# Filter products moved from POOL to VectorE, x loaded first, and additions, norms and routing of the first half rearranged in a two-layer attention and mixture-of-experts kernel

## The chip, the cores and the metric

One core of a Trainium2 chip runs the whole program. Its engines are TensorE (PE; PEld are its weight loads), VectorE (DVE), ScalarE (ACT), GpSimd (POOL) and SyncE (SP), which issues most DMAs. The metric is the device time of one execution in microseconds, less is better. Three runs of the kernel before took 493.38, 490.51 and 492.42 us, the median is 492.42.

## The reference

Two layers on x of 4 x 1024 x 128, all float32. Cut to what matters:

```python
xn = layernorm(x)
x = x + attention(xn, w_q, w_k, w_v) + moe_top1(xn, wg, W, b)      # layer 0
xn = layernorm(x)
x = x + conv(xn, Wu, Wv, W1, W2, W3, Wo) + moe_top2(xn, Wg, W1, W2) # layer 1
```

Attention is causal, with rotated q and k, one head of 128, four sequences of 1024. `moe_top1` sends each token to the best of 8 experts (128x128 each, 512 tokens at most), `moe_top2` to the best two of 8 experts (128 to 256 to 128, relu). `conv` is a long convolution over 1024 positions by FFT: `y = (xn Wu + bu) * irfft(rfft(xn Wv + bv) * rfft(h))`, then `Wo`. Its filter h comes from positions alone, h = gelu(gelu(pos W1 + b1) W2 + b2) W3 + b3 with a decay, where gelu(v) is taken as 0.5 v (1 + tanh(c (v + 0.0447 v^3))).

## The kernel before

The 4096 tokens are 32 tiles of 128 (`NT`), 8 per sequence (`J`), and `i` or `n` is mostly a tile. Every engine has one program written out by hand; they meet only at semaphores, and each engine takes its instructions in order. Nothing is scheduled by a planner: tables of row numbers at the top of the file (lines 165 to 184 and 226 to 227) say behind which row of attention a piece of other work stands.

Prelude. SP loads x in four groups, the constants, `wvg` (weights of values and of layer 0's gates), the transform matrices `mats`, `wqk`, `rope`, layer 0's expert weights and biases, and then fills the DRAM tables `slots0`, `moe0` and `slots1` with markers (L702, L707). VectorE takes statistics of each group and writes normalized rows (L1482, L1485, L1491); between them POOL computes the inverse deviation by a power (`inverse_std`, L798 and L800). PE transposes the rows, ACT copies them to `xT`, PE multiplies by `wvg`, ACT copies values and gate logits out (`take_values`). The filter's two hidden layers are spread over the prelude: PE multiplies (`filter_layer`), ACT makes a biased copy and a square (L956, L959), POOL makes `ht = ht*hx + hx` as a multiplication and an addition (`times_x_plus_x`, L847), ACT the tanh (L963), POOL `hg = hg*hx + hx`; that is four times two POOL instructions of 64x1024. Then VectorE runs `routing0`: one-hots of the best expert, the count of earlier tokens by two matmuls on PE (`routing_counts`), the slot of each token (`slot0`, last written at L1546).

Rows. With the slots POOL scatters the 32 tiles of rows to `slots0` (`scatter_rows`, L826), one indirect DMA each, waiting after every second. Meanwhile PE, ACT and VectorE go through attention, row block n = 0 to 31: PE `scores(n+1)`; VectorE `row_max(n+1)` (L1713, L1717); ACT `exp_rows(n+1)` (L1010); PE `transpose_probs(n)` (L1263); ACT and VectorE copy them (L1020, L1725); PE `weigh_values(n-1)`; VectorE `attention_row(n-1)` adds to x (L1731). Rotated q and k of the next sequence come in between (`project` on PE, `rotate` on VectorE), and so do pieces of other work:

- The filter's last layer at row 2, its radix pass on VectorE (`radix_forward`) in rows 3 to 5, its spectrum on PE (`filter_spectrum`, 64 matmuls in two rows) in rows 6 and 7.
- Layer 0's experts from row `MOE0_FROM` = 8: when all 32 scatters are in, SP loads the sorted rows (L715) into a ring of 16, PE transposes and multiplies (L1297, L1305), VectorE adds the bias (L1739), POOL sends each tile back to its tokens (`send_back`, L836). When all 32 are back, SP loads them (`y0`, L736).
- From row 21 on VectorE adds them to x and takes statistics for the second norm, tile by tile (`add_tiles`, L1747, L1751, L1755; `ADD_BEFORE_MAX` and `ADD_BEHIND_ROW`). POOL computes the deviations of groups 0 to 2 right away (L880 to L888). ACT writes normalized rows of these groups (`norm_rows`, L1027, `NORM_AT`), PE transposes them (`transpose_norms`, L1281) and multiplies by the gate weights (`gates`, `GATES_AT`). The last group's rows are written by VectorE (L1491), four and four.
- The first half of the tokens (tiles 0 to 15) is routed to layer 1's experts in pieces between rows 26 and 28 (`routing1`, 30 steps). After it POOL scatters them with `dispatch` (L813): 16 tiles for the best expert, new ids (`second_ids`, L822), 16 tiles for the second best. In front of dispatches 4 and 12 of this scatter stand the two halves of the last group's deviation (`NORM_IN_SCATTER`, four tiles each).

After the rows PE works off a list, `conv_at(PRELUDE)`: projections of the convolution, `("vu", k)`, five of them, then the transposes of the last group's normalized rows, three more projections, that group's gates, four projections, the counts of the second routing, the rest, and eight forward transforms. VectorE has, in this order: the last group's second four rows (`norm_rows(2 * B - 1, J // 2, J // 2)`, waiting for `rstd_done`), ten steps of the first radix pass, the second half's routing up to its one-hots, the rest of the radix pass, the rest of the routing, eight spectral products. POOL scatters the second half of the tokens: 12 dispatches (`SCATTER_IN_PRELUDE`) ahead of the expert rounds, two per round later. SP loads rows for the rounds once the first half's scatter is in. Then come 40 rounds of a pair of expert tiles each, with the inverse transforms between them, and a tail that adds everything and stores.

## Time and profile before

| | before |
|---|---|
| median of three runs | 492.42 us |
| the profiled execution | 493.04 us |
| its span, first to last instruction | 491.2 us |
| mean granted clock of PE | 0.934 of full |
| PE busy | 366.0 us, 75% |
| PEld busy | 298.7 us, 61% |
| VectorE busy | 294.4 us, 60% |
| POOL busy | 258.4 us, 53% |
| ACT busy | 225.9 us, 46% |

Busy shares are averages over stages that have different limits, and the idle time of an engine that isn't the bottleneck costs nothing. "Idle before <-releaser" in a row tells how long the engine had stood still before the instruction and whose work ended that wait. Matmul ends are modelled, and POOL's spans are rough. All helper matmuls have one line, L1161, so they are told apart by their tiles.

### The profile page before, as it was taken

To read this page: it belongs to the slowest core of one execution; us is meant where nothing else is said; L and a number is where in the kernel's file an instruction comes from. 1 tells how busy PE (TensorE), PEld (TensorE's weight loads), DVE (VectorE), ACT (ScalarE), POOL (GpSimd) and SP (SyncE) were. 2 spreads that over 40 slices of the span, in tenths; PEclk is the share of its full clock that TensorE was granted. 3 is DMA by queue.
4 is the path that set the end of the run, shared out by engine and by line. 5 is a ranking of instruction groups with operands and counts; after the bars stand their busy time and mean duration, and the time that the engine had idled before them with its cause. 6 is when DMAs were issued, how large, how long until landed. Compare 5 with 4: busy or idle time off the path is not lost.

```text
span 491.2 us, 7805 instructions
## 1 busy us (share of the span) xinstructions
PE 366.0 (75%) x2302; PEld 298.7 (61%) x2302; DVE 294.4 (60%) x782; ACT 225.9 (46%) x551; POOL 258.4 (53%) x254
## 2 busy tenths in 40 slices
PE   2485588869997975949997978898887777766720
PEld 0272255658675644737996867787776667755620
DVE  3977569614773796474688993478438772244105
ACT  1373042325332316334343066434567676687724
POOL 2754766733666323016566676666666555365540
PEclk9999599997998999687998999999999999999975
DMA  9999999823321330001111282445322215422407
GB/s 211 396 197 262 166 140 135 268 51 85 87 75 40 111 89 1 1 5 39 34 34 37 69 261 75 142 140 151 112 69 75 63 29 158 137 74 74 126 11 252
DMA packets 64744, 55.05 MB, mean 112 GB/s; under 512 B 6819, under 2 KB 56683, under 8 KB 64446
## 3 DMA queue, kind: packets, MB, share of 16 engines
q1 hardware_dynamic: 57888, 41.71, 35.6%
q0 software_dynamic: 6656, 12.51, 8.4%
q10 hardware_dynamic: 158, 0.33, 0.4%
q8 instruction: 19, 0.31, 0.3%
q14 instruction: 23, 0.19, 0.1%
HBM read 30.44 MB, written 25.27 MB: 113 GB/s over the span
## 4 chain that ended last, share of the span: by engine, by line
PE 44%; issue 13%; ACT 12%; DVE 10%; DMA 10%; POOL 8%; SPq 1%; ACTq 0%; POOLq 0%; DVEq 0%
PE psS L1161 19%; PE psO L1161 15%; PE psT L1161 7%; ACT hT L1122 7%; POOL slots L826 4%; DMA slots<-row,slot 4%; DMA moe<-ys,xs 2%; POOL w L847 2%; DMA xres<-in_x 2%; ACT row L1027 1%; PE psT L1263 1%; POOL moe L836 1%; DVE work L1713 1%; DVE xres L1747 1%; DMA moe<-ys,ring 1%
## 5 line engine op out<-in xcount | busy, mean ns | idle before, releaser
L813 POOL DMA_INDIRECT slots<-row,slot x64 | 69.3, 1083 | 57.0 <-DVE slot L1580 22.4
L836 POOL DMA_INDIRECT moe<-ys,xs x61 | 61.1, 1001 | 58.3 <-issue 16.6
L1161 PE MATMUL psO<-ring,hT 128*128 128x128 f32 x320 | 45.2, 284 | 45.1 <-ACT hT L1122 45.1
L1161 PEld LDWEIGHTS psO<-ring,hT 128*128 128x128 f32 x320 | 38.7, 191 | 53.4 <-issue 53.4
L1122 ACT ACTIVATE hT<-psT,ring 128x128 f32<-128x128 f32 x160 | 45.6, 368 | 45.7 <-PE psT L1161 45.7
L1868 DVE TENSOR_TENSOR ys<-psO,ring 128x256 f32<-128x256 f32 x40 | 17.0, 424 | 75.3 <-PE psO L1161 75.1
L1055 ACT ACTIVATE ring<-w 128x642 f32 x80 | 55.9, 761 | 1.1 <-issue 1.0
L1161 PE MATMUL psS<-work 128*128 128x512 f32 (+3 forms) x96 | 42.6, 558 | 12.6 <-DVE work L1696 8.8
L836 POOL DMA_INDIRECT moe<-ys,w x35 | 38.0, 1087 | 23.3 <-DVE ys L1868 9.7
L1020 ACT ACTIVATE work<-psT 128x512 f32<-128x512 f32 (+3 forms) x32 | 16.5, 516 | 66.6 <-PE psT L1263 66.6
L826 POOL DMA_INDIRECT slots<-row,slot x32 | 34.9, 1091 | 18.1 <-DMA slots<-row,slot 10.9
L1161 PE MATMUL psT<-xsT,ring 128*128 128x128 f32 x320 | 42.3, 275 | 0.5 <-ACT xsT L1115 0.5
L1161 PEld LDWEIGHTS psT<-xsT,ring 128*128 128x128 f32 x320 | 39.9, 192 | 1.3 <-ACT xsT L1115 0.7
L1161 PE MATMUL psO<-work 128*128 128x128 f32 x288 | 39.7, 286 | 0.0
L1010 ACT ACTIVATE work<-psS,work 128x128 f32<-128x128 f32 (+7 forms) x32 | 23.7, 739 | 34.7 <-DVE work L1717 34.4
L1713 DVE TENSOR_REDUCE work<-psS 128x1 f32<-128x128 f32 (+7 forms) x32 | 24.0, 750 | 25.5 <-PE psS L1161 23.9
L1161 PEld LDWEIGHTS psO<-work 128*128 128x128 f32 x288 | 37.1, 203 | 0.0
L1161 PEld LDWEIGHTS psS<-work 128*128 128x128 f32 x96 | 17.9, 214 | 27.5 <-issue 18.5
L1263 PE MATMUL psT<-cst,work 128*128 128x128 f32 x144 | 24.0, 298 | 14.3 <-ACT work L1010 14.3
L1161 PE MATMUL psS<-xT,work 128*128 128x512 f32 x64 | 31.1, 628 | 1.3 <-ACT work L1010 1.3
L1263 PEld LDWEIGHTS psT<-cst,work 128*128 128x128 f32 x144 | 17.0, 153 | 23.2 <-ACT work L1010 18.3
L1161 PE MATMUL psS<-work,mats 128*128 128x256 f32 x128 | 30.1, 395 | 0.0
(272 smaller groups left out, 781.4 us busy)
## 6 DMA issues: line engine op xcount, KB each, us to landing
slots<-xs SPq DMA_DIRECT2D x14, 516.0 KB, 14.7
mats<-in_iv SPq DMA_DIRECT2D x16, 256.0 KB, 3.7
xs<-slots SPq DMA_DIRECT2D x61, 64.5 KB, 1.9
w<-in_w SPq DMA_DIRECT2D x8, 321.0 KB
w<-slots SPq DMA_DIRECT2D x35, 64.5 KB, 1.9
xres<-in_x SPq DMA_DIRECT2D x4, 512.0 KB, 9.7
mats<-in_fw SPq DMA_DIRECT2D x1, 2048.0 KB, 11.3
moe<-xs SPq DMA_DIRECT2D x4, 512.0 KB, 7.8
```

Of the source, the lines that this page charges most:

```text
L813: pool.indirect_dma_start(slots1[:, :], bass.IndirectOffsetOnAxis(ap=(slot1, slot2)[k][:, i:i + 1], axis=0), row[:, i, :], None, bounds_ch ...
L826: pool.indirect_dma_start(dst[:, :], bass.IndirectOffsetOnAxis(ap=slots[:, i:i + 1], axis=0), row[:, i, :], None, bounds_check=bound, oob_ ...
L836: pool.indirect_dma_start(dst[:, :], bass.IndirectOffsetOnAxis(ap=row_slots[l][m][:, D:ROWW].bitcast(I32), axis=0), ys[:, n % UNROLL, :], ...
L847: pool.tensor_tensor(t[0:FO, :], t[0:FO, :], hx[0:FO, :], op).then_inc(f_pool, 1)
L1010: act.activation(prob[n % 2][:, 0:(i + 1) * P], S[n % 2][:, :, :].rearrange("p a m -> p (a m)")[:, 0:(i + 1) * P], ACT.Exp, bias=negmax[:, ...
L1020: act.activation(pT[n % 2][:, 0:k, :].rearrange("p j q -> p (j q)"), t_bank("p", n, 0)[:, 0:k * P], ACT.Copy).then_inc(pt_act, 1)
L1055: act.activation(pair_w[p % RING_PAIRS][:, t, :], w12[:, bass.ds(e, 1), :].rearrange("p e h -> p (e h)"), ACT.Copy).then_inc(e_w, 1)
L1122: last = act.activation(hT[:, k, :], TP[1][:, k * P:(k + 1) * P], ACT.Relu, bias=pair_w[p % RING_PAIRS][:, k // 2, B1_AT + k % 2:B1_AT + k ...
L1161: return pe.matmul(o, lhsT, rhs, start=start, stop=stop)
L1263: last = pe.transpose(t_bank("p", n, c)[:, (j - 4 * c) * P:(j - 4 * c + 1) * P], prob[n % 2][:, j * P:(j + 1) * P], ident)
L1713: dve.tensor_reduce(negmax[:, n:n + 1], S[n % 2][:, :, :].rearrange("p a m -> p (a m)")[:, 0:(n % J + 1) * P], X, ALU.max, negate=True).th ...
L1868: tt(ys[:, m:m + 2, :], O[p % 2][:, 0:2 * D].rearrange("p (t d) -> p t d", d=D), pair_w[p % RING_PAIRS][:, :, B2_AT:W_COLS], ALU.add).then ...
```

## The change

The two filter layers leave the prelude. PE's matmuls for them, ACT's three activations and the products now stand in rows 0 to 4 (`FILT_AT`), and the products are four fused instructions on VectorE, (ht + 1) * hx and (hg + 1) * hx. Radix pass and spectrum follow in rows 6 to 8 and in rows 9 and 10, the experts of layer 0 start at row 9. SP loads all of x before `wvg`, puts `w0`, its biases and the matrices behind the first fills, and layer 1's weights behind the first 16 loads of sorted rows, the second eight of which now wait for the filter's radix pass. PE makes projection (0,0) between token groups 1 and 2, VectorE rotates it and takes row 0's maximum in the middle of the first routing. At the other end the additions of tiles 0 to 15 come in two blocks of eight, those of 16 to 23 move to rows 26 and 27, norms of groups 0 and 1 stand in rows 22 and 23, their transposes ahead of the row's own (`TOKENS_AT`), gates in rows 23 and 24; the first half's routing has 12 steps behind row 24, 10 behind row 25 and the rest ahead of row 27's maximum. On POOL the third group's norm and both halves of the last one stand in front of dispatches 6, 14 and 24 of the scatter, and 20 dispatches of the second half stand ahead of the rounds.

```diff
-FILT_RADIX_AT, FILT_DFT_AT = 3, 6
-
-SPLIT_AT = 9
-GATES_AT = (24, 25, 29)
-NORM_AT = {23: [(0, 0), (0, 1)], 24: [(1, 0), (1, 1)], 27: [(2, 0)], 28: [(2, 1)]}
-COUNTS_AT = 27
+FILT_AT = (0, 2)
+FILT_RADIX_AT, FILT_DFT_AT = 6, 9
+
+SPLIT_AT = 12
+TOKENS_AT = (23, 24, 29)
+GATES_AT = (23, 24, 29)
+NORM_AT = {22: [(0, 0), (0, 1)], 23: [(1, 0), (1, 1)], 28: [(2, 0), (2, 1)]}
+COUNTS_AT = 25
...
-MOE0_FROM = 8
+MOE0_FROM = 9
...
-ADD_BEFORE_MAX = {22: (4, 8), 23: (12, 16), 25: (20, 24), 29: (24, 28), 31: (28, 30)}
-ADD_BEHIND_ROW = {21: (0, 4), 22: (8, 12), 24: (16, 20)}
-ROUTING_BEFORE_MAX = {26: 6, 28: 8}
-ROUTING_BEHIND_ROW = {26: 6, 27: 10, 28: R1_STEPS}
+ADD_BEFORE_MAX = {22: (8, 16), 27: (20, 24), 29: (24, 28), 31: (28, 30)}
+ADD_BEHIND_ROW = {21: (0, 8), 26: (16, 20)}
+ROUTING_BEFORE_MAX = {26: R1_STEPS}
+ROUTING_BEHIND_ROW = {24: 12, 25: 10}
...
-SCATTER_IN_PRELUDE, SCATTER_PIECES = 12, 2
-NORM_IN_SCATTER = (4, 12)
+SCATTER_IN_PRELUDE, SCATTER_PIECES = 20, 2
+NORM_IN_SCATTER = (6, 14, 24)
...
-                    sp.dma_start(wvg, wvg_in).then_inc(w_a_loaded, 16)
-            sp.dma_start(mats[:, :, :, :], fw_in).then_inc(fw_loaded, 16)
+            sp.dma_start(wvg, wvg_in).then_inc(w_a_loaded, 16)
             sp.dma_start(wqk, wqk_in).then_inc(rope_loaded, 16)
             sp.dma_start(rope, rope_in).then_inc(rope_loaded, 16)
-            sp.dma_start(w0[:, :, :], w0_in).then_inc(moe0_w_loaded, 16)
-            sp.dma_start(y0.rearrange("p j d -> p (j d)"), b0_in.rearrange("e d -> (e d)").partition_broadcast(P)).then_inc(moe0_w_loaded, 16)
-            sp.dma_start(bias[:, :], bvuo_in.partition_broadcast(P)).then_inc(bias_loaded, 16)
...
             fill_slots(0, slots0, TILES0)
             for i in range(0, NT, 8):
                 sp.dma_start(moe0[i * P:(i + 8) * P, :].rearrange("(i p) w -> p i w", p=P),
                              xs[:, :, 0:D]).then_inc(moe0_filled, 16)
+            sp.dma_start(mats[:, :, :, :], fw_in).then_inc(fw_loaded, 16)
             fill_slots(1, slots1, TILES1)
...
-            sp.wait_ge(rad_f, RAD_F)
-            for a, b in [(w12[:, e, :], w12_in[e]) for e in range(E)] + [
-                    (wv[:, :], wv_in), (wu[:, :], wu_in), (wg1[:, :], wg1_in), (wo[:, :], wo_in)]:
-                sp.dma_start(a, b).then_inc(l1_w_loaded, 16)
-
-
             sp.wait_ge(slots_filled[0], 16 * TILES0 // 8)
             sp.wait_ge(moe0_filled, 16 * NT // 8)
             sp.wait_ge(slots_filled[1], 16 * TILES1 // 8)
             sp.wait_ge(sent0, 16 * NT)
             for n in range(TILES0):
+                if n == UNROLL:
+                    sp.wait_ge(rad_f, RAD_F)
                 load_rows(0, slots0, n)
+                if n == RING[0] - 1:
+                    for a, b in [(w12[:, e, :], w12_in[e]) for e in range(E)] + [
+                            (wv[:, :], wv_in), (wu[:, :], wu_in), (wg1[:, :], wg1_in), (wo[:, :], wo_in)]:
+                        sp.dma_start(a, b).then_inc(l1_w_loaded, 16)
...
-            inverse_std(0)
-            inverse_std(1)
-            filter_cubic(0)
-            inverse_std(2)
-            inverse_std(3)
-            filter_gelu(0)
-            filter_cubic(1)
-            filter_gelu(1)
+            for g in range(B):
+                inverse_std(g)
...
-            for g in range(B - 1):
+            def second_norm(g):
+
                 tiles = slice(J * g, J * g + J)
                 inverse_std(B + g)
...
 
+            second_norm(0)
+            second_norm(1)
             pool.wait_ge(ids_done, 2)
             pool.wait_ge(xn_done, NT + NT // 2)
             pool.wait_ge(slots_filled[1], 16 * TILES1 // 8)
             pool.wait_ge(slot1_ready, 2)
+            def norms_in_scatter(j):
+
+                if j == NORM_IN_SCATTER[0]:
+                    second_norm(2)
+                if j in NORM_IN_SCATTER[1:]:
+                    inverse_std(2 * B - 1, J // 2 * (NORM_IN_SCATTER.index(j) - 1), J // 2)
+
             for i in range(HT):
-                if i in NORM_IN_SCATTER:
-                    inverse_std(2 * B - 1, J // 2 * NORM_IN_SCATTER.index(i), J // 2)
+                norms_in_scatter(i)
                 dispatch(0, 0, i)
             for g in range(2):
                 second_ids(0, g)
             pool.wait_ge(ids_done, 4)
             for i in range(HT):
+                norms_in_scatter(HT + i)
                 dispatch(0, 1, i)
...
             exp_rows(0)
             for n in range(NT):
+                if n in TOKENS_AT:
+                    g = TOKENS_AT.index(n)
+                    for u in (2 * g, 2 * g + 1):
+                        take_transposed(u, t_bank("t", u))
                 take_pt(n)
                 if n + 1 < NT:
                     exp_rows(n + 1)
+                if n in FILT_AT:
+                    act.wait_ge(filt_loaded, 32)
+                    filter_layer(FILT_AT.index(n))
+                if n - 1 in FILT_AT:
+                    filter_tanh(FILT_AT.index(n - 1))
...
-            pe.wait_ge(filt_loaded, 32)
-            filter_layer(0)
             pe.wait_ge(cst_loaded, 16)
             pe.wait_ge(w_a_loaded, 16)
             for g in range(B):
                 transpose_tokens(g)
                 values_and_gates(g)
+                if g == 1:
+                    pe.wait_ge(rope_loaded, 32)
+                    project(0, 0)
             pe.wait_ge(casts_done, 3)
             pe.wait_ge(ones_done, 2)
-            filter_layer(1)
+            scores(0)
             pe.wait_ge(vg_free, 16)
             routing_counts(0, O[0])
-            pe.wait_ge(rope_loaded, 32)
-            pe.wait_ge(f_act, 4)
-            project(0, 0)
-            pe.wait_ge(rt, R0_CUM)
-            scores(0)
+            pe.wait_ge(filt_loaded, 32)
             for n in range(NT):
                 for b, h in projections_at(n):
                     project(b, h)
                 if n + 1 < NT:
                     scores(n + 1)
+                if n in FILT_AT:
+                    filter_layer(FILT_AT.index(n))
+                if n in TOKENS_AT:
+                    g = TOKENS_AT.index(n)
+                    for u in (2 * g, 2 * g + 1):
+                        wait_emptied(pe, T_USES, T_AT[("t", u)])
+                        transpose_norms(u, t_bank("t", u))
                 transpose_probs(n)
                 if n == FILT_RADIX_AT - 1:
                     filter_layer(2)
                 if n in (FILT_DFT_AT, FILT_DFT_AT + 1):
                     for u in range(2):
                         filter_spectrum(2 * (n - FILT_DFT_AT) + u)
+                if n == 1:
+                    pe.wait_ge(rt, R0_CUM)
                 if n:
                     weigh_values(n - 1)
...
+            def filter_cubic(k):
+                dve.wait_ge(f_act, 3 * k + 2)
+                stt(ht[0:FO, :], ht[0:FO, :], 1.0, hx[0:FO, :], ALU.add, ALU.mult).then_inc(f_dve, 1)
+
+            def filter_gelu(k):
+                dve.wait_ge(f_act, 3 * k + 3)
+                stt(hg[0:FO, :], hg[0:FO, :], 1.0, hx[0:FO, :], ALU.add, ALU.mult).then_inc(f_dve, 1)
...
+            norm_stats(0)
+            norm_stats(1)
+            norm_rows(0)
+            norm_stats(2)
+            norm_rows(1)
+            norm_stats(3)
+            norm_rows(2)
+            norm_rows(3)
 
             def rotate(b, h):
 
@@ -1761,12 +1762,21 @@
 
             dve.wait_ge(rope_loaded, 32)
             rotate(0, 0)
+            dve.wait_ge(vg_free, 16)
+            dve.wait_ge(cst_loaded, 16)
+            first_layer_routing = routing0()
+            take(first_layer_routing, R0_OH)
+            row_max(0)
+            finish(first_layer_routing)
...
             for n in range(NT):
                 for b, h in projections_at(n):
                     rotate(b, h)
+                if n - 1 in FILT_AT:
+                    filter_cubic(FILT_AT.index(n - 1))
+                if n - 2 in FILT_AT:
+                    filter_gelu(FILT_AT.index(n - 2))
```

Not shown: PE's, ACT's and the bank tables' bookkeeping, by which the filter's two layers use score bank 0 in turn with the rows and the transposes take their banks ahead of the row's.

## Rows read from the trace of the kernel before

**Rows 1.** The page's chain that ended last, shares of the span by engine.

```profile
PE 44%; issue 13%; ACT 12%; DVE 10%; DMA 10%; POOL 8%; SPq 1%; ACTq 0%; POOLq 0%; DVEq 0%
```

**Rows 2.** Groups by line, POOL, 0 to 54 us: count, busy us and mean ns, idle before.

```profile
L847 POOL TENSOR_TENSOR w<-w 64x1024 f32<-64x1024 f32 x8 | 18.7, 2339 | 11.5 <-ACT w L959 10.0 <-ACT w L963 1.2
```

**Rows 3.** Timeline, 0 to 56 us: start us, us, instruction, idle before and releaser.

```profile
38.34 0.59 DVE L1513 TENSOR_REDUCE m<-lg 128x32 f32<-128x256 f32 x1 [4.77 <-ACT lg L951]
...
41.62 3.60 PE L1161 MATMUL psS<-xT,work 128*128 128x512 f32 x8
...
44.94 2.07 DVE L1542 SCALAR_TENSOR_TENSOR tables<-tables 128x256 f32<-128x256 f32 x1
...
47.50 0.42 DVE L1544 SCALAR_TENSOR_TENSOR tables<-tables 128x256 f32<-128x256 f32 x1
...
48.58 1.69 DVE L1546 TENSOR_SCALAR slot<-best 128x32 int32<-128x32 f32 x1
...
52.84 1.52 POOL L826 DMA_INDIRECT slots<-row,slot  x1 [0.19 <-issue]
```

**Rows 4.** Timeline of PE, 88 to 120 us.

```profile
97.62 3.81 PE L1161 MATMUL psT<-hspec,mats 128*128 128x128 f32 x32 [0.34 <-ACT work L1020]
...
108.83 0.45 PE L1297 MATMUL psT<-cst,xs 128*128 128x128 f32 x1 [3.44 <-DMA xs<-slots]
```

**Rows 5.** Timeline of POOL, 100 to 265 us, the sends back.

```profile
117.53 0.97 POOL L836 DMA_INDIRECT moe<-ys,xs  x1 [11.91 <-DVE ys L1739]
...
164.74 0.97 POOL L836 DMA_INDIRECT moe<-ys,ring  x1 [0.30 <-issue]
```

**Rows 6.** Timeline of DVE, 118 to 200 us, additions and maxima.

```profile
171.81 1.13 DVE L1747 SCALAR_TENSOR_TENSOR xres<-work,gate,xres 128x128 f32<-128x128 f32 x4
...
177.49 1.13 DVE L1747 SCALAR_TENSOR_TENSOR xres<-work,gate,xres 128x128 f32<-128x128 f32 x4
...
179.60 1.19 DVE L1713 TENSOR_REDUCE work<-psS 128x1 f32<-128x1024 f32 x1
...
185.88 0.26 DVE L1713 TENSOR_REDUCE work<-psS 128x1 f32<-128x128 f32 x1
```

**Rows 7.** Timeline of DVE, 197 to 292 us, the first routing's first step.

```profile
204.08 0.37 DVE L1513 TENSOR_REDUCE m<-lg 128x16 f32<-128x128 f32 x1 [3.50 <-ACT lg L1036]
```

**Rows 8.** Timeline of POOL, 100 to 265 us, the second scatter.

```profile
218.78 1.12 POOL L813 DMA_INDIRECT slots<-row,slot  x1 [22.37 <-DVE slot L1580]
...
240.27 0.23 POOL L798 TENSOR_SCALAR veps<-mv 128x4 f32<-128x4 f32 x1 [2.87 <-DVE mv L1755]
240.65 1.04 POOL L800 TENSOR_TENSOR rstd<-veps,cst 128x4 f32<-128x4 f32 x1
...
248.24 0.42 POOL L822 COPY row<-cst 128x8 int32<-128x8 int32 x1
```

**Rows 9.** Timeline of DVE, 236 to 252 us.

```profile
241.73 1.12 DVE L1491 TENSOR_SCALAR row<-xres,mv,rstd 128x128 f32<-128x128 f32 x4 [1.65 <-POOL rstd L800]
...
251.96 0.37 DVE L1513 TENSOR_REDUCE m<-lg 128x16 f32<-128x128 f32 x1 [1.48 <-ACT lg L1036]
```

**Rows 10.** Timeline of PE, 197 to 292 us.

```profile
244.88 1.04 PE L1281 MATMUL psS<-cst,row 128*128 128x128 f32 x8
...
249.76 1.85 PE L1161 MATMUL psS<-wg,xT 128*128 128x8 f32 x16
...
281.08 0.40 PE L1417 MATMUL psT<-cst,xs 128*128 128x128 f32 x2
```

**Rows 11.** Timeline of SP, 80 to 290 us.

```profile
278.53 1.80 SPq L715 DMA_DIRECT2D xs<-slots  x4
```

**Rows 12.** Timeline of PE, 118 to 200 us, gates after an idle stretch.

```profile
194.20 3.55 PE L1161 MATMUL psO<-wg,xT 128*128 128x8 f32 x16 [3.44 <-ACT xT L1032]
```

**Rows 13.** Windows: stretch, us, busy us of PE, PEld, DVE, ACT, POOL, granted clock, DMA, GB/s.

```profile
194.00:196.00 2.00, 1.80 (x9) 1.83 (x9) 0.00 (x0) 0.54 (x2) 1.81 (x2) 0.51 0.00 0
```

**Rows 14.** Timeline of POOL, 70 to 93 us.

```profile
81.78 1.93 POOL L826 DMA_INDIRECT slots<-row,slot  x1 [0.78 <-DMA slots<-row,slot]
```

57 lines of the change are left out of this document (15 added, 42 removed).

## Prediction

> **What bounds the kernel now.** I read first the page's chain that ended last [rows 1]: TensorE (PE) and its hand-overs carry most of it, and POOL's scatter with its DMAs a good tenth. That is an average over stages, so I walked the chain in order of time and looked in each stage, on each engine's timeline, for the wait that ends last.
>
> Up to 53 us POOL decides. It has eight filter products of 2.34 us, 18.7 us in all [rows 2]; the last two stand in front of the first scatter at 52.84 [rows 3]. VectorE suffers too: L1542 takes 2.07 us where L1544, of the same shape, takes 0.42, and L1546 takes 1.69 for 32 columns; both end about when a POOL product ends [rows 3]. From 52.84 it is the scatter of 32 tiles; PE, idle for 3.44 us, gets the first sorted rows at 108.83 [rows 4], 56.0 us after its start. From 117.53 to 166 POOL sends 32 tiles back, (164.74-117.53)/31 = 1.52 us each [rows 5]; the additions begin right behind, at 171.81 [rows 6]. From there VectorE, ScalarE (ACT) and PE alternate: additions, norms, gates, then from 204.08 [rows 7] the routing of the first half, up to the second scatter at 218.78, for which POOL had waited 22.4 us [rows 8]. Then PE makes projections and forward transforms, with the second routing on VectorE (from 251.96 [rows 9]) across it, and goes into the expert rounds at 281.08 [rows 10]; SP had begun to load their rows at 278.53 [rows 11]. Two paths arrive there nearly together. The rounds and the tail aren't changed in what they compute, so what moves 281.08 moves the end.
>
> **The prelude.** The eight POOL products go. VectorE makes four fused ones of 64x1024 instead, each about 1.2 us by the nearest row, L1713 with 1024 columns, 1.19 [rows 6] (bounds 1.0 and 2.3). For PE two things cancel: ACT no longer holds the first token group back behind a filter product (about 4.5 us), but the eight matmuls of projection (0,0), 3.60 [rows 3], now stand between groups 1 and 2, and the weights of the values land behind all of x, which can cost 0 to 1.5. So the routing, which began at 38.34 [rows 3], begins at about 38. Its 11.9 us until the last slot is written (38.34 to 50.2) lose 2.07-0.42 = 1.6, some 1.5 of L1546 and a wait of 1.0 for ACT's exponential, and gain 0.45 for the maximum of row 0: 8.2 us, slots at 46.2, scatter at 46.3 instead of 52.84 [rows 3]. That is 6.5 us (bounds 4 and 9). With the same 56.0 for the scatter (52.8 if it keeps 1.52 a tile) the sorted rows reach PE at 102.3.
>
> **Rows 0 to 10.** Attention starts some 9.8 us earlier. The two filter layers go through ACT, VectorE and PE in turn (square, product, tanh, product, matmul) and stretch rows 1 to 4 by about 5 us. That is covered, since PE otherwise waits for the sorted rows; if the cover is gone, it costs up to 5. Not covered is the filter spectrum: half of it, 32 matmuls in 3.81 us [rows 4], now stands in row 10, between the arrival of expert 0's rows and its result. First send-back: 117.53 [rows 5] minus 6.5 plus 3.8 and 0.6 for a larger row = 115.4. POOL's 32 sends at 1.52 set the rest, so the additions come 2.1 earlier, and 0.7 more for what was left of slack behind row 21: 169.0. Of the 6.5 us less than half is left. The weights of layer 1, moved behind the first 16 row loads on SP's queue, land by 120 and are wanted by gates only; the fills moved ahead of the transform matrices delay nobody before row 9. Both cost nothing as long as SP's queue is that far ahead (0 to 2).
>
> **Rows 21 to 26.** Additions come in two blocks of 8 tiles, 4.2 us each (four tiles with statistics take 179.60-177.49 = 2.1 [rows 6]). With the rotation between them ((177.49-171.81)-2.1 = 3.6) and 1.4 for the maximum: 169.0 + 13.4 = 182.4. From the maximum of row 24 (185.88 [rows 6]) to the routing (204.08 [rows 7]) the kernel before has 18.2 us, with two norm groups on ACT and two gates; after needs about 16, because additions and the third norm are not in between: 198.4. The routing took 204.08 to 218.78 = 14.7, with a wait and two rows' attention work inside; in nearly one piece about 11.1. So the second scatter starts at P = 209.5, 9.3 us earlier (bounds 197, if also the spectrum is covered, and 214).
>
> **Rows 27 on, where the gain goes.** The last tile group's norm on POOL stands inside the scatter. Before, its second half stood in front of dispatch 12: POOL had waited 2.87 us for the statistics, computed at 240.65 for 1.04 [rows 8], and VectorE wrote the last four normalized tiles at 241.73, having waited 1.65 [rows 9]. Now it stands in front of dispatch 24, and POOL takes things in order. Its time is P + 24 x 1.52 = 36.5, plus the third norm at dispatch 6 (2.4 net), plus the first half of the last norm at 14 (1.0 net), plus the two copies of ids that start at 248.24 in [rows 8] (2.3 net) = P + 42.2; result 1.4 later, P + 43.6 = 253.1. Row 31 is through by about 240 as before, since its maximum is held by the third norm, now in the scatter too, and by the gates; so the statistics lie ready for 12 us. Behind that wait stands all of VectorE: the four tiles, the first radix pass, the second routing, the products. PE stands behind it too, for after five projections it transposes those tiles: 244.88 [rows 10] becomes 253.6, and the last ends at P + 45.1 = 254.6 instead of 245.9, +8.7. From there to the gates' result it has projections and 16 gate matmuls, and comes to them idle. Before, after an idle 3.44 us, 16 such matmuls took 3.55 [rows 12] with a granted clock of 0.51, the level of 1.2 GHz [rows 13], where they take 1.85 at the full clock [rows 10]; I add 2.3 (bounds 0 and 4). The second routing, from 251.96 [rows 9], starts at 263. From there VectorE had no gap up to the products, so 281.08 becomes 292. POOL's 9.3 us turn into slack: SP could load rows at about 265, and PE comes at 292. Twenty dispatches of the second half ahead of the rounds instead of twelve leave POOL about as far behind the results as now: 0 (bounds -1 and 2).
>
> **Sum.** The profiled execution took 493.04 us with a span of 491.2: 493.0 + 8.7 + 2.3 = 504.0, some 503.5 beside the median 492.42, which lies 0.6 lower.
>
> **A rule that speaks against the change.** A dispatch on POOL takes 0.97 us at best and 1.93 at 81.78, while VectorE runs additions and products on SBUF [rows 14]. The Trainium skill, SBUF — State Buffer, "SBUF: two separate sides", says that the port pair which VectorE and GpSimd share is an exclusive lock, and that a DMA from POOL can be starved of its descriptors by it. By that rule, moving the products beside the scatter only changes who is blocked; the row agrees, with at most 1 us for a product.
>
> **Rivals.**
> (a) Faster: POOL starts so early that dispatch 24 comes when the statistics do. The point from which it decides is P + 45.1 = 245.9, P = 200.8; with P at 195 to 198 both paths into 281 come 3 to 6 us earlier: 487 to 490. For it: eight products gone and two stretched VectorE instructions [rows 2, 3]. Against: it wants the low end of every bound at once. 0.13.
> (b) No change: P between 198 and 203 and no stretched gates, 490 to 495. 0.10.
> (c) The forecast: the stall behind dispatch 24, 495 to 508. 0.65.
> (d) Worse: each of the four products holds a dispatch by up to 1.93-0.97 = 0.96 [rows 14], 3.8 us, and the filter chain stretches rows 1 to 9 past 102 us; P 213 or later: 508 to 512. 0.12. That the change doesn't do what it says belongs here: if the products were not on the scatter's path, P would stay and the stall grow; [rows 3] speaks against it.
>
> **Numbers.** Forecast 503.5. A measurement of this kernel tells about 0.5%, 2.5 us, from no change. Faster by more than that is (a), 0.13; within it is (b) with a little of (c), 0.12; slower 0.75. The range 491 to 509 leaves out (a) and part of (d) and (b).
>
> **What would show it.** No L847 on POOL, the first scatter near 46, first send-back near 115, additions near 169, second scatter near 210. Then the point that decides: POOL's last power of 128x4 near 253 with no wait ahead of it, VectorE's normalization waiting for it some 12 us, PE idle before its transposes of those tiles, rounds from about 292. If the wait on POOL's rstd is under 3 us, the forecast is wrong in its sign; if the first scatter starts after 50, in its first step.

## The result and the profile after

The kernel after took 502.87 us in its profiled execution and 509.42, 512.43 and 513.27 in three more, the kernel before 490.51 to 494.95 in four: 2.64% slower, with an interval of 2.10% to 3.18%, a ratio that sets the two longest executions of the kernel after aside as disturbed. Below, every kernel with the old front part stays within 5.3 us over its executions. Most of those with the new one spread over 7 to 11 us; norm18 and front_only fall into two groups some 8 to 9 us apart, most of the others also have times in between. So the spread belongs to the kernels, and the experiments ask for its reason. By the ratio the time after is about 505 us, inside the range of the forecast; the median of all four, 510.9, lies 1.9 above it; the profiled execution lies 0.6 below the forecast of 503.5 (1.1 below the 504.0 that the sum gave for a profiled one).

The page of after, its line of busy times and the granted clock in 40 slices:

```profile
span 501.1 us, 7803 instructions
...
PE 371.0 (74%) x2302; PEld 300.4 (60%) x2302; DVE 289.8 (58%) x786; ACT 226.5 (45%) x551; POOL 241.2 (48%) x246
...
PEclk9995899999998879679879999999999999999985
```

The span grew from 491.2 to 501.1. Now the stages, in order of time. Timelines (start us, us, instruction, idle before and releaser), first of the prelude and the first scatter. PE in the kernel before, a row that no group above holds:

```profile
22.55 4.08 PE L1161 MATMUL psO<-work,xT 128*128 128x136 f32 x16 [6.17 <-ACT xT L939]
```

All engines in the kernel after, 0 to 56 us:

```profile
15.75 3.18 PE L1153 MATMUL psO<-work,xT 128*128 128x136 f32 x16
...
33.94 0.58 DVE L1510 TENSOR_REDUCE m<-lg 128x32 f32<-128x256 f32 x1 [4.65 <-ACT lg L940]
...
41.80 0.18 DVE L1543 TENSOR_SCALAR slot<-best 128x32 int32<-128x32 f32 x1
...
42.98 1.23 POOL L831 DMA_INDIRECT slots<-row,slot  x1 [19.46 <-DVE slot L1543]
```

The values of the first token group come 6.8 us earlier, since ACT no longer holds them behind a filter tanh that itself waited for POOL's product; projection (0,0) takes 3.6 of that back; the first routing starts 4.4 us earlier than in [rows 3], its last slot is written in 0.18 us instead of 1.69, and the first scatter starts 9.9 us earlier (52.84 in [rows 3]).

PE in after, its first transpose of sorted rows:

```profile
100.75 0.30 PE L1290 MATMUL psT<-cst,xs 128*128 128x128 f32 x1
```

POOL in after, the first send-back and the second scatter:

```profile
111.05 0.97 POOL L841 DMA_INDIRECT moe<-ys,xs  x1 [14.60 <-DVE ys L1740]
...
207.49 1.11 POOL L818 DMA_INDIRECT slots<-row,slot  x1 [27.47 <-DVE slot L1577]
```

VectorE in after, the first addition and the first half's routing:

```profile
165.14 2.19 DVE L1748 SCALAR_TENSOR_TENSOR xres<-work,gate,xres 128x128 f32<-128x128 f32 x8 [1.14 <-DMA work<-moe]
...
195.81 0.37 DVE L1510 TENSOR_REDUCE m<-lg 128x16 f32<-128x128 f32 x1 [1.64 <-ACT lg L1021]
```

PE no longer waits for the first sorted rows (3.44 us in [rows 4]): attention now comes to them no earlier than they arrive, so of the 9.9 us 6.5 reach the first send-back [rows 5], 6.7 the additions [rows 6], 8.3 the first half's routing [rows 7], and 11.3 the second scatter [rows 8]. Here the kernel is ahead by 11 us. Then POOL's timeline of after, 225 to 262 us:

```profile
249.26 0.23 POOL L803 TENSOR_SCALAR veps<-mv 128x4 f32<-128x4 f32 x1 [0.15 <-issue]
249.64 1.04 POOL L805 TENSOR_TENSOR rstd<-veps,cst 128x4 f32<-128x4 f32 x1
...
252.34 6.36 POOL L818 DMA_INDIRECT slots<-row,slot  x1 [0.30 <-issue]
```

All engines in after, 236 to 262 us:

```profile
238.13 0.18 DVE L1756 BATCH_NORM_AGGREGATE mv<-stats 128x2 f32<-128x6 f32 x1
...
250.72 1.12 DVE L1487 TENSOR_SCALAR row<-xres,mv,rstd 128x128 f32<-128x128 f32 x4 [12.41 <-POOL rstd L805]
...
251.21 1.16 PE L1274 MATMUL psS<-cst,row 128*128 128x128 f32 x4 [7.48 <-DVE row L1487]
...
258.02 1.85 PE L1153 MATMUL psS<-wg,xT 128*128 128x8 f32 x16
...
260.22 0.37 DVE L1510 TENSOR_REDUCE m<-lg 128x16 f32<-128x128 f32 x1 [2.36 <-ACT lg L1021]
```

PE in after, at the start of the rounds:

```profile
289.31 0.38 PE L1413 MATMUL psT<-cst,xs 128*128 128x128 f32 x2
...
297.59 1.05 PE L1153 MATMUL psT<-xsT,ring 128*128 128x128 f32 x8
```

The last tile's statistics are ready at 238.3. POOL takes them at 249.26, with no wait of its own: it had been busy with the 24 dispatches in front. VectorE stands still for 12.41 us and writes the last rows at 250.72 instead of 241.73 [rows 8, 9], PE transposes them at 251.21 (in [rows 10] together with the first four at 244.88), the second routing starts 8.3 us later than in [rows 9] and the rounds 8.2 us later than in [rows 10]. SP had begun to load their rows at 269.79, far ahead (278.53 in [rows 11]). The whole lead of POOL is gone, and 8 us with it.

### The profile page after: what moved, and what is told of

Its sections match the earlier page's. It is cut to its first block and busy times, and to the rows that moved or that the text cites. A ratio compares the mean times of both kernels' runs of the same rounds, so it can differ in the third digit from the quotient of the medians.

```text
span 501.1 us, 7803 instructions
## 1 busy us (share of the span) xinstructions
PE 371.0 (74%) x2302; PEld 300.4 (60%) x2302; DVE 289.8 (58%) x786; ACT 226.5 (45%) x551; POOL 241.2 (48%) x246
## 5 line engine op out<-in xcount | busy, mean ns | idle before, releaser
L818 POOL DMA_INDIRECT slots<-row,slot x64 | 72.1, 1127 | 68.8 <-DVE slot L1577 35.5
L1114 ACT ACTIVATE hT<-psT,ring 128x128 f32<-128x128 f32 x160 | 45.7, 368 | 47.5 <-PE psT L1153 47.5
L1153 PE MATMUL psO<-work 128*128 128x128 f32 x288 | 41.4, 295 | 0.0
L995 ACT ACTIVATE work<-psS,work 128x128 f32<-128x128 f32 (+7 forms) x32 | 23.7, 740 | 35.1 <-DVE work L1718 35.0
L1153 PEld LDWEIGHTS psO<-work 128*128 128x128 f32 x288 | 39.1, 212 | 0.0
L1256 PE MATMUL psT<-cst,work 128*128 128x128 f32 x144 | 25.8, 313 | 13.3 <-ACT work L995 12.4
L1256 PEld LDWEIGHTS psT<-cst,work 128*128 128x128 f32 x144 | 18.1, 160 | 24.4 <-ACT work L995 16.2
L1153 PE MATMUL psS<-xT,mats 128*128 128x256 f32 x128 | 29.2, 380 | 1.4 <-DMA mats<-in_fw 1.4
```

The source lines that it names most:

```text
L818: pool.indirect_dma_start(slots1[:, :], bass.IndirectOffsetOnAxis(ap=(slot1, slot2)[k][:, i:i + 1], axis=0), row[:, i, :], None, bounds_ch ...
L995: act.activation(prob[n % 2][:, 0:(i + 1) * P], S[n % 2][:, :, :].rearrange("p a m -> p (a m)")[:, 0:(i + 1) * P], ACT.Exp, bias=negmax[:, ...
L1114: last = act.activation(hT[:, k, :], TP[1][:, k * P:(k + 1) * P], ACT.Relu, bias=pair_w[p % RING_PAIRS][:, k // 2, B1_AT + k % 2:B1_AT + k ...
L1153: return pe.matmul(o, lhsT, rhs, start=start, stop=stop)
L1256: last = pe.transpose(t_bank("p", n, c)[:, (j - 4 * c) * P:(j - 4 * c + 1) * P], prob[n % 2][:, j * P:(j + 1) * P], ident)
```

## The experiments

Theory A: the loss is VectorE's wait behind dispatch 24. Its rival B: it comes from the front part (filter in the rows, order of the transfers) or from 20 dispatches ahead of the rounds. Later runs asked for more: D, that PE's idle stretches let its clock fall in the first rows and make the long executions; E, that the spread has another cause; F, that it is the filter's chain through ACT, VectorE and PE itself; G, that POOL's longer queue costs time in the rounds; K, that the products count wherever they stand in POOL's queue.

One table of the profiled executions (us from the start; "last rows" is VectorE's last write of normalized rows, "rounds" PE's first transpose of their rows):

```
kernel            first scatter  send-back  additions  2nd scatter  last rows  rounds   span
before                52.84       117.53     171.81      218.78      241.73    281.08   491.2
after                 42.98       111.05     165.14      207.49      250.72    289.31   501.1
norm18                44.18       119.03     173.45      214.65      250.87    291.26   501.8
before_norm20         52.11       115.48     169.41      218.40      252.61    291.77   501.8
front_only            44.68       118.99     173.40      215.53      240.87    280.26   493.1
late_only             52.47       116.92     171.17      216.21      259.61    298.28   510.1
front_busy            46.08       112.12     166.71      208.65      233.99    274.42   484.4
front_filt04          43.40       109.01     167.27      209.19      230.41    269.73   481.3
after_busy            44.79       113.74     168.29      210.87      254.19    292.82   506.3
after_prelude12       43.70       118.26     172.66      215.51      258.73    297.61   507.5
filt04_busy           45.10       111.98     169.98      213.35      238.68    279.14   489.0
filt04_busy_wvg       43.97       113.40     171.54      214.97      240.31    280.80   490.6
products_on_pool      44.12       128.50     186.83      228.76      254.11    294.67   504.5
before_busy           53.16       116.72     172.24      219.38      241.14    280.49   492.3
```

From the last rows to the end it is 248.8 to 252.2 us in all fourteen. What moves "last rows" moves the time, to within those 3.4 us; the second scatter doesn't (207.49 in after, 218.78 in before).

**norm18.**

```diff
-NORM_IN_SCATTER = (6, 14, 24)
+NORM_IN_SCATTER = (6, 14, 18)
```

> The kernel after, with one number changed: the second half of the last group's norm stands in front of dispatch 18 of the scatter instead of 24. In the profile after, the statistics it needs were ready at 238.2 us and the new ids were written at 236.3, so the power can be computed near 240.3 instead of 249.64, and VectorE writes the last rows near 242 instead of 250.72. Theory A (the loss is the wait behind dispatch 24): the second routing begins near 252 (260.22 after, 251.96 before), the rounds near 281 (289.31 after, 281.08 before), and the profiled execution takes 493 to 496 us, that is a ratio to the kernel before of 0.998 to 1.008. Theory B (the loss comes from the other edits: the filter in rows 0 to 10, the order of the DMAs, or 20 dispatches ahead of the rounds): the wait moves, but the time stays at 503 or more, ratio 1.02 or more. Theory C (both half): 498, ratio 1.01.

495.49 us median of 13 (493.74 to 505.17): nine executions at 493.7 to 495.8, for which the ratio is 1.0026, interval 1.0011 to 1.0041, and four at 503.5 to 505.2. A holds: moving one instruction pair by six dispatches takes some 8 us from the short group (502.9 with 24) and 6 to 8 from the long one (509 to 513). The profiled execution is a long one, 503.57, so its last rows are no earlier than in the profile of after; the long profile with 24, that of after_prelude12 below, has them at 258.73. The wait is back to the 1.65 us of [rows 9], in VectorE's timeline of norm18:

```profile
250.87 1.12 DVE L1487 TENSOR_SCALAR row<-xres,mv,rstd 128x128 f32<-128x128 f32 x4 [1.65 <-POOL rstd L805]
```

**before_norm20.** The kernel before, second half of the last norm at dispatch 20 instead of 12.

```diff
-NORM_IN_SCATTER = (4, 12)
+NORM_IN_SCATTER = (4, 20)
...
+                if HT + i in NORM_IN_SCATTER:
+                    inverse_std(2 * B - 1, J // 2, J // 2)
                 dispatch(0, 1, i)
```

> The kernel before, with the second half of the last group's norm moved from dispatch 12 to dispatch 20 of the same scatter, and nothing else. The scatter begins at 218.78; 20 dispatches of 1.52 us, the first half of the norm (1.0) and the two copies of ids (2.3) put the power at 252.5 and its result at 253.9, where it was 241.7. Theory A: VectorE waits some 12 us more for it, the last rows come 12 us later, and all but the slack of 1.65 goes into the time: 10 to 12 us, ratio 1.020 to 1.025, without any other part of the change. Theory B: PE has projections and transforms of its own that fill the wait, so less than 3 us is lost, ratio under 1.006.

503.85 us (501.47 to 504.88), ratio 1.021, interval 1.0183 to 1.0237. A again, without any other edit, at the size that the count of dispatches gave. Timeline of before_norm20:

```profile
251.53 1.04 POOL L800 TENSOR_TENSOR rstd<-veps,cst 128x4 f32<-128x4 f32 x1
252.61 1.12 DVE L1493 TENSOR_SCALAR row<-xres,mv,rstd 128x128 f32<-128x128 f32 x4 [12.94 <-POOL rstd L800]
```

**late_only.** The kernel before with after's tables of additions, norms, gates and routing, and its POOL order (6, 14, 24; 20 dispatches ahead).

> The late part of the change alone: the kernel before with additions in two blocks, norms and gates of groups 0 and 1 and the routing of the first half as in the change, the third norm and the two halves of the last one in front of dispatches 6, 14 and 24, and 20 dispatches ahead of the rounds; the prelude, the filter and the DMAs are those of the kernel before, and the transposes of the normalized rows stay behind their row's own. In the profile after, the second scatter began 42.4 us behind the first addition, here 171.81 + 42.4 = 214.2 (218.78 before). The power behind dispatch 24 is computed at 214.2 + 42.2 = 256.4. Theory A: VectorE writes the last rows at 257.5, some 16 us later than the 241.73 of before, less 1.7 of slack: ratio 1.026 to 1.032, 505 to 508 us, the worst of all four, since the front part no longer pays back 6.7 us. Theory B (the front part is the harmful one): ratio 1.005 or less.

512.06 us (511.68 to 514.82), ratio 1.0393, interval 1.0368 to 1.0418: A's direction, and 4 to 7 us more than it gave. The stall is 10.35 us. What I had missed is that the second scatter came 2.0 us later than assumed and the power with it (POOL's power at 258.53 instead of 256.4), that no slack was left to take off, and that 20 dispatches cost 1.7 behind the rounds' start. The last rows are 17.9 us later than in [rows 9] and 1.0 more is added behind them, which makes the 18.9 us by which the span grew. Only 8.7 of the 17.9 are the wait (10.35 instead of 1.65): the last statistics are ready at 249.3, where they were at 240.1, so some 9 us go to the rearranged rows themselves. Timeline of late_only:

```profile
233.12 3.55 PE L1171 MATMUL psO<-wg,xT 128*128 128x8 f32 x16
...
259.61 1.12 DVE L1501 TENSOR_SCALAR row<-xres,mv,rstd 128x128 f32<-128x128 f32 x4 [10.35 <-POOL rstd L800]
```

The gates of the third group, at 233.12, show the low clock's 3.55 us that [rows 12] had.

**front_only.** The whole change with the late tables, the POOL order (4, 12) and 12 dispatches of the kernel before; only the transposes of the normalized rows still stand ahead of their row's own, as in after.

> The front part of the change alone: filter layers in rows 0 to 4 with products on VectorE, x loaded first, order of the DMAs, experts from row 9; additions, norms, gates, routing of the first half, the places of the norms in the scatter and 12 dispatches ahead of the rounds are those of the kernel before. Theory A (the front part is a gain that reaches the end once nothing else is moved): the additions begin near 165.1 us as in the profile after (171.81 before), the second scatter 47.0 us behind them, at 212.1 (218.78 before), the rounds some 6 us earlier than 281.08, near 275, and the time is 486 to 488 us, ratio 0.987 to 0.992. Theory B (the products of VectorE beside the scatter, or the moved transfers, cost later what the start gained): ratio 1.00 or more, with the additions early but the rounds not before 280.

483.85 us once, 492.17 to 494.88 five times. The gain that A gave (486 to 488) was passed once and missed five times, and the profiled execution tells why: the first scatter is 8.2 us early, but the first send-back is 1.5 us later than before (118.99). PE comes to the sorted rows at 110.06 with no wait for them, though their transfer was issued at 97.38. Windows (stretch, us, busy us of PE, PEld, DVE, ACT, POOL, granted clock, DMA, GB/s) first of front_only, then of after:

```profile
60.00:65.00 5.00, 3.80 (x10) 1.69 (x8) 0.35 (x1) 2.02 (x4) 3.14 (x4) 0.50 1.15 167
65.00:70.00 5.00, 4.82 (x16) 3.72 (x17) 2.30 (x5) 2.51 (x6) 3.21 (x4) 0.50 1.23 188
```

After:

```profile
60.00:65.00 5.00, 3.61 (x12) 2.35 (x12) 2.36 (x3) 2.56 (x4) 3.31 (x4) 0.51 1.26 147
65.00:70.00 5.00, 5.00 (x18) 2.59 (x17) 2.74 (x8) 2.31 (x4) 3.14 (x4) 1.00 1.25 172
```

Both leave the prelude with a granted clock of 0.50 after PE's idle 3.3 us, and stand idle again for 3.6 us in front of the second filter layer. In front_only the clock then stays at 0.50, the 1.2 GHz level, up to 70 us, in after it is back at 65. Row 5's result comes at 95.14 in front_only and 87.21 in after, and that distance of 8 us is kept to the additions (173.40 and 165.14). Some 2.0 of the 8 were there at row 0's result (55.48 and 53.44), where the first scatter was also 1.7 later; the other 5.9 arise in rows 1 to 5, which take, from row 0's result to row 5's, 33.8 us in after and 39.7 in front_only. norm18 and after_prelude12, the other profiles of long executions, take 39.8 and show 0.50 in both windows too; the kernel before takes 30.2. VectorE's results of rows 0 and 5 in front_only:

```profile
55.48 0.33 DVE L1731 SCALAR_TENSOR_TENSOR xres<-psO,work,xres 128x128 f32<-128x128 f32 x1
...
95.14 0.34 DVE L1731 SCALAR_TENSOR_TENSOR xres<-psO,work,xres 128x128 f32<-128x128 f32 x1
```

And in after:

```profile
53.44 0.33 DVE L1732 SCALAR_TENSOR_TENSOR xres<-psO,work,xres 128x128 f32<-128x128 f32 x1
...
87.21 0.34 DVE L1732 SCALAR_TENSOR_TENSOR xres<-psO,work,xres 128x128 f32<-128x128 f32 x1
```

**front_busy.** front_only with PE kept busy through both idle stretches by matmuls that nobody reads.

```diff
+                if k == 1:
+                    for h in range(5):
+                        mm(S[0][0:FO, h % 2, :], f1w, pe_sb[0:FO, 512 * (h % 2):512 * (h % 2) + 512])
                 if k:
                     pe.wait_ge(f_dve, 2 * k)
...
+            for h in range(6):
+                mm(O[0][:, :], wqk[:, h % 4, :], xT[:, 0:512])
             routing_counts(0, O[0])
```

> The front part alone, as in front_only, plus eleven idle-time matmuls on PE whose results nobody reads: six of 128x512 in front of the first routing's counts, where PE stood idle for 3.32 us in the profile after, and five of 64x512 in front of the second filter layer, where it stood idle for 3.55 us. What was seen: front_only took 483.85 us once and 492.2 to 494.9 in five other executions, and its profiled one (494.88) had additions at 173.4 us where the profile after had them at 165.1; the granted clock is 0.50 from 58 to 70 us there and comes back to 1.00 at about 66 us in the profile after. Theory D (PE's two idle stretches let its clock fall to 1.2 GHz in rows 0 to 5, and the front part has left no slack to hide it): with PE busy through them the granted clock is 1.00 from 36 to 80 us, the additions begin at 162 to 165, and all executions lie together at 480 to 485 us, ratio 0.972 to 0.984. Theory E (the spread has another cause, as the DMA queues or POOL): it stays, some executions near 484 and most near 493, and the matmuls cost up to 2 us more.

486.32 us (482.78 to 487.42, six executions), ratio 0.9853, interval 0.9816 to 0.989. D holds in kind: the clock is 1.00 where it was 0.50 (below; only from 47.5 to 50 us it is 0.50), rows 1 to 5 take 34.0 us again, additions are at 166.71, no execution is above 487.4. The median is 1.3 us above D's band: the six matmuls made PE 2.1 us late for the counts (40.78 instead of 38.67) and the first scatter 1.4 later. It is the steadiest of the kernels with the new front part, and it beats both the kernel before and the kernel after.

The same windows of front_busy:

```profile
60.00:65.00 5.00, 3.85 (x14) 1.47 (x12) 0.35 (x1) 1.56 (x4) 3.05 (x4) 1.00 1.22 159
65.00:70.00 5.00, 4.36 (x20) 2.62 (x21) 2.50 (x6) 3.36 (x6) 3.61 (x4) 1.00 1.20 192
```

**front_filt04.** front_only with the second filter layer two rows later.

```diff
-FILT_AT = (0, 2)
-FILT_RADIX_AT, FILT_DFT_AT = 6, 9
-SPLIT_AT = 12
+FILT_AT = (0, 4)
+FILT_RADIX_AT, FILT_DFT_AT = 8, 10
+SPLIT_AT = 13
```

> The front part alone, with the second filter layer at row 4 instead of 2, the radix pass at rows 8 and 9 and the spectrum at rows 10 and 11. PE no longer waits 3.55 us for the product of the first layer, which is made in row 2; in its place stand two more rows between them. The rest is that of front_only. Theory D: one of the two idle stretches is gone, so fewer executions show the low clock in rows 1 to 5: additions near 164 to 167, most executions at 482 to 486 us, perhaps some at 492. Theory E: as many executions near 493 as with front_only. Theory F (the chain through ACT, VectorE and PE itself is what stretches the rows, not the clock): 2 to 3 us faster than front_only in every execution, 481 and 490, with the same distance between the two.

487.08 us (483.14 to 493.99, nine), ratio of six of them 0.9894, interval 0.9861 to 0.9926. Nearer to D than to E: six lie at 483 to 489, three at 491 to 494. F, 2 to 3 us off every execution, is not seen: the long ones take 491.0 to 494.0, against 492.2 to 494.9 of front_only.

**after_busy.** The whole change with the eleven matmuls.

> The whole change with the same eleven idle-time matmuls on PE. The kernel after took 502.87 us in its profiled execution and 509.4 to 513.3 in three others. Theory D: the granted clock is 1.00 from 36 to 80 us, the additions begin at 162 to 165, and every execution lies at 498 to 504 us, with the wait of VectorE behind dispatch 24 as before (power at P + 42.2, 9 to 13 us of idle time): ratio 1.012 to 1.022. Theory E: median 508 to 512, as without them.

507.97 us (502.25 to 509.1, six), ratio 1.0269, interval 1.0219 to 1.0319: D missed by 4 us, and the median lies where E's band begins. Two executions took 502.3 and 504.1, four 507.9 to 509.1. So with the late part in place the matmuls don't close the spread. In the profiled one the clock is 0.96 or more from 35 to 45 us, but 0.79 from 80 to 85; the first scatter is 1.8 us later than in after, additions are at 168.29, and the wait behind dispatch 24 is still 12.40 us. Of its span's 5.2 us over after's, 3.5 are there before the last rows and 1.7 behind them.

**filt04_busy.** front_filt04 with four matmuls in front of the counts.

> front_filt04 with four matmuls of 128x512 that nobody reads in front of the first routing's counts, where PE stands idle for 3.3 us. In the profile of front_filt04 (span 481.3) the granted clock was 0.79 from 35 to 40 us, 0.50 from 40 to 45 and 0.69 from 45 to 50, and of nine executions three took 491 to 494 us, the others 483 to 489. Theory D (idle stretches of PE let the clock fall, and what is left of the spread hangs on this one): granted clock 0.95 or more from 35 to 45 us, no execution over 488, median 482 to 485, ratio 0.978 to 0.986. Theory E (the spread has another cause): a third of the executions stays above 490, and the median at 487.

490.28 us (483.49 to 493.44, twelve), half of them above 490: D as I had put it fell. One early gap is gone by the filter's place, the other is filled, and the clock does stay at 1.00 from 30 to 45 us. It falls later instead, in rows 6 to 10, and lower than in front_filt04's profiled execution (from 85 to 90 us 0.60 where that has 1.00). Windows of filt04_busy, and in the last line the stretch behind the second scatter's start:

```profile
100.00:105.00 5.00, 3.83 (x15) 2.73 (x14) 3.73 (x14) 2.23 (x6) 0.00 (x0) 0.50 0.21 51
...
210.00:225.00 15.00, 8.96 (x37) 7.95 (x38) 8.75 (x34) 5.47 (x12) 8.38 (x10) 0.58 0.09 28
```

And of front_filt04, with PE's first transpose of sorted rows in front:

```profile
96.90 1.73 PE L1289 MATMUL psT<-cst,xs 128*128 128x128 f32 x4 [5.33 <-DMA xs<-slots]
...
100.00:105.00 5.00, 5.00 (x34) 4.87 (x33) 0.92 (x3) 1.75 (x4) 0.00 (x0) 0.73 0.74 189
...
210.00:225.00 15.00, 12.48 (x81) 10.46 (x82) 9.01 (x36) 7.87 (x16) 10.43 (x12) 0.82 0.13 41
```

So no single idle stretch is the cause. Of the 8.3 us between the last rows of these two profiles 2.7 are there at the additions; 5.6 arise behind them, in rows 21 to 31, where the clock from 210 to 225 us is 0.58 and not 0.82. front_filt04's profile is also the exception there: from the additions to the last rows it takes 63.1 us, where front_only, front_busy, filt04_busy and filt04_busy_wvg take 67.3 to 68.8. And not every low clock is paid for: in the same profile it is 0.50 from 40 to 45 us, yet PE waits 5.33 us for the first sorted rows at 96.90. What holds is weaker than D: a low clock costs time only where no other wait covers it, as in rows 1 to 5 of front_only and, it seems, behind the additions. What decides where it falls is open.

**before_busy.** The kernel before with sixteen such matmuls in its own idle stretch from 45 to 54 us.

> The kernel before with sixteen matmuls of 128x512 that nobody reads behind projection (0,0), where PE stood idle from 45.2 to 54 us and showed a granted clock of 0.50 from 48 to 60 us. Nothing else. Theory D has two halves, and this tells the second: the low clock costs the kernel before nothing, since its rows 0 to 7 wait for the scatter anyway (PE idle for 3.44 us before the first sorted rows at 108.83). So the granted clock from 50 to 60 us rises to 1.00 and the time stays within 0.4% of the kernel before, 490 to 494 us. Against it: if the clock there is on the path, 4 to 6 us faster, ratio 0.987 to 0.992.

493.6 us (491.42 to 496.65), ratio 1.001, interval 0.9985 to 1.0034. The clock rises and the time stays: in the kernel before PE waits for the first sorted rows anyway, still 0.57 us at 110.37 here. The window of before:

```profile
55.00:60.00 5.00, 4.17 (x8) 1.65 (x8) 1.00 (x5) 1.20 (x5) 3.14 (x4) 0.50 1.28 169
```

And of before_busy:

```profile
55.00:60.00 5.00, 5.00 (x13) 2.17 (x12) 0.00 (x0) 0.00 (x0) 3.14 (x4) 1.00 1.28 185
```

**filt04_busy_wvg.** filt04_busy with `wvg` loaded behind the first group of x again.

> filt04_busy with one line of the transfers as in the kernel before: the weights of the values are loaded behind x's first group and the constants instead of behind all of x. In the profile after PE began its transposes of x at 13.98 us, on their landing, where VectorE had begun to write the normalized rows at 12.44. Expected if that wait is a cost: transposes of the first group at 12.6 to 13, the routing's first step 0.5 to 1.4 us earlier than with filt04_busy, the first scatter as much earlier, and the time the same or up to 1 us less, since attention and not the scatter sets the first send-back. If not: x's later groups land later by the 68 KB in front of them, and the routing begins at the same time within 0.3 us.

490.12 us (484.0 to 492.42), ratio 0.9906, interval 0.9866 to 0.9946. The routing starts at 34.91 instead of 36.03 and the first scatter 1.13 us earlier, inside what was expected; the time is the same (490.28). x first costs 1.1 us in the prelude; at the end nothing shows in a spread of 8 us.

**products_on_pool.** front_filt04 with the products made by POOL, in front of dispatches 4, 6, 20 and 24.

```diff
+            def product_in_scatter(i):
+                if i in (4, 20):
+                    pool.wait_ge(f_act, (2, 5)[i == 20])
+                    times_x_plus_x(ht)
+                if i in (6, 24):
+                    pool.wait_ge(f_act, (3, 6)[i == 24])
+                    times_x_plus_x(hg)
```

> front_filt04 with the four filter products made by POOL again, each as a multiplication and an addition of 64x1024, in front of dispatches 4, 6, 20 and 24 of the first scatter; VectorE makes none. The filter stands in the rows as in front_filt04. Theory K (what counts is that the products leave POOL's queue, not only the prelude): 8 x 2.34 = 18.7 us more for the scatter, its last dispatch near 111 us (92.6 in front_filt04), the first send-back at 123 to 128 (109.0), additions near 181 (167.3), and 494 to 502 us, ratio 1.00 to 1.02. Theory L (leaving the prelude is enough, for the scatter had slack against attention in rows 0 to 9): the first send-back at most 5 us later, and under 490 us.

503.69 and 506.26 us, ratio 1.0246, interval 1.0199 to 1.0292. K, and more than it gave: the last dispatch is at 112.14 (92.59 in front_filt04), additions 19.6 us later than in front_filt04. The last rows are 23.7 later, but the 4.1 us between are no price of the products: from the additions to the last rows it takes 67.3 us, as front_only does. The medians are 17.9 us apart. POOL's timeline of products_on_pool:

```profile
49.73 2.33 POOL L833 TENSOR_TENSOR w<-w 64x1024 f32<-64x1024 f32 x1
...
112.14 0.97 POOL L849 DMA_INDIRECT slots<-row,slot  x1 [0.30 <-issue]
```

**after_prelude12.** The whole change with `SCATTER_IN_PRELUDE = 12`.

> The whole change with 12 instead of 20 dispatches of the second half ahead of the expert rounds, as in the kernel before. In the profile after, the first send-back of the rounds was at 312.26, 14.0 us behind the first result at 298.25 (9.4 us in the profile of before), and the span grew by 1.7 us more between the start of the rounds and the end than in the profile of before. Theory G (POOL's queue, longer by eight dispatches, is what adds these 1.7 us): the first send-back comes 9 to 10 us behind the first result and the rounds and the tail together take 210.1 us again, from the first transpose of the rounds' rows on PE to the end (211.8 in the profile after). Theory H (the 1.7 us have another cause): they take 211.5 or more, though POOL is less behind.

509.35 us, one execution. Its profile is that of a long one (rows 1 to 5 take 39.8 us, sorted rows at 109.33, second scatter at 215.51). From the first transpose of the rounds to the end: 209.9 us, G's 210.1 and not after's 211.8; the first send-back is 1.72 us behind the first result instead of 14.0. From the second round's transposes (297.59 in after) to the end it is 203.5, 202.5, 203.5 and 205.4 us in the four kernels with 20 dispatches ahead (after, norm18, late_only, after_busy) and 201.6 to 202.0 in all ten with 12. So twenty cost 0.5 to 3.8 us, and G holds. Timeline of after_prelude12:

```profile
306.55 0.42 DVE L1878 TENSOR_TENSOR ys<-psO,ring 128x256 f32<-128x256 f32 x1
...
308.27 2.08 POOL L841 DMA_INDIRECT moe<-ys,xs  x1 [5.50 <-issue]
```

## Why the prediction was right, and where it was not

**What bounds the kernel, and the first scatter.** Right in its row, wrong in its size: 9.9 us, forecast 6.5 with an upper bound of 9. The mis-sized term is the start of the routing, 33.94 where I had 38: the first token group's values came 6.8 us earlier, where I took 4.5 less up to 1.5 for `wvg`. The stretch from there to the last slot was right (8.0 us, forecast 8.2), and so were the products, 1.21 us each (forecast 1.2). products_on_pool shows that taking them out of POOL's queue is worth 18 to 20 us once the filter stands in the rows.

**Their price beside the scatter.** Rival (d) had allowed 3.8 us. In after, POOL dispatches of 1.35, 1.49 and 1.15 us instead of 0.97 lie beside the first three products and one of 0.97 beside the fourth: 1.1 us in all. Not all of that is the products' either: the dispatch of 50.55 ran beside additions of the rotation, and the product began 1.04 us behind it. Other profiles show more for a single product, up to 2.03 us in norm18 (dispatch at 76.36, product at 76.33), so (d)'s price per product can occur. The direction is that of the Trainium skill, SBUF — State Buffer, "SBUF: two separate sides", by which a DMA from POOL can be starved of its descriptors through the port pair that VectorE and GpSimd share; the rows agree in direction, and no run shows that this lock is the reason. Behind the last norm, beside the radix pass, one dispatch takes 6.35 to 6.37 us in five profiles (after, before_norm20, late_only, after_busy, after_prelude12); in norm18, beside the same pass, three take 1.28, 1.44 and 2.25, so the pass alone doesn't set it. In after it costs nothing, since POOL then waits 8.06 us for VectorE's slots at 276.39.

POOL in after, two of the dispatches:

```profile
50.55 1.35 POOL L831 DMA_INDIRECT slots<-row,slot  x1 [0.30 <-issue]
...
55.71 1.49 POOL L831 DMA_INDIRECT slots<-row,slot  x1 [0.78 <-DMA slots<-row,slot]
```

VectorE in after, the products beside them:

```profile
51.59 1.21 DVE L1492 SCALAR_TENSOR_TENSOR w<-w 64x1024 f32<-64x1024 f32 x1
...
55.13 1.22 DVE L1496 SCALAR_TENSOR_TENSOR w<-w 64x1024 f32<-64x1024 f32 x1 [1.36 <-ACT w L952]
```

**Rows 0 to 10.** This step failed. I wrote that the stretch of rows 1 to 4 "is covered, since PE otherwise waits for the sorted rows; if the cover is gone, it costs up to 5". The cover was 3.44 us, and the 9.9 us by which the scatter came earlier used it up. In the profiled execution just so (the rows' transposes at 100.75, no wait); in front_only and norm18 PE comes 9.3 us later still. The size of the stretch was wrong as well: rows 1 to 5 take 3.6 us more than before in after's profile (33.8 and 30.2), but 9.5 in the profiles of long executions, because the low clock comes on top, which the prediction had not reckoned with here. That is the likely reason why the median went above the range: three of four executions of after took 509 to 513, and of those there is no profile; after_prelude12, the same but for the 12 dispatches, took 509.35 and shows it.

**The first send-back and the additions.** Forecast 115.4 and 169.0, measured 111.05 and 165.14; the spectrum's 3.8 us in row 10 did come in between, but 4 us more had been won before.

**Rows 21 to 26.** Forecast 198.4 for the routing and P = 209.5, measured 195.81 and 207.49; from the additions at 165.14 the two steps took 1.3 and 0.6 us longer than their terms.

**The wait behind dispatch 24.** Right in place, mechanism and size: power at P + 42.15 (forecast P + 42.2), a wait of 12.41 us (forecast 12), the last rows 9.0 us later than before. PE's last transposes end at 252.37, 6.4 us later than before; the forecast had 8.7, and the difference is P, 2.0 earlier than forecast. norm18 and before_norm20 show the wait from both sides. The statistics at "about 240 as before" were 238.3, 1.8 us earlier than before, though the additions had begun 6.7 earlier: the third norm at dispatch 6 and the routing in one piece hold rows 27 to 31. norm18 against front_only, with additions at 173.4 in both, prices that without the wait. Timeline of norm18, third group's rows on ACT and row 31's maximum on VectorE:

```profile
225.96 3.18 ACT L1012 ACTIVATE row<-xres,veps,rstd 128x128 f32<-128x128 f32 x8 [1.77 <-POOL veps L868]
...
240.39 1.22 DVE L1714 TENSOR_REDUCE work<-psS 128x1 f32<-128x1024 f32 x1 [6.58 <-PE psS L1153]
```

The same two in front_only:

```profile
217.51 1.64 ACT L1011 ACTIVATE row<-xres,veps,rstd 128x128 f32<-128x128 f32 x4
...
230.39 1.23 DVE L1713 TENSOR_REDUCE work<-psS 128x1 f32<-128x1024 f32 x1 [6.58 <-PE psS L1152]
```

ACT's rows of the third group come 8.5 us later and row 31's maximum 10.0 us later, so the last rows do too (250.87 and 240.87), though the second scatter started 0.9 us earlier. The late part loses some 10 us even with the wait gone; P was won by giving away the rows that P doesn't need.

**The gates' clock.** Forecast +2.3, and near in size for another group of matmuls. The gates of 258.02 take 1.85 us, the full clock. But PE had stood idle for 7.48 us, and the projections that it made first, between the transposes and the gates, ran at a granted clock of 0.50: a pair of them took 0.74 us instead of 0.44. From the end of the transposes to the start of the second routing it is 7.85 us in after and 6.04 before, so 1.8 us were paid there. Window and PE's timeline of after:

```profile
252.50:255.00 2.50, 2.50 (x13) 2.25 (x13) 2.50 (x4) 0.54 (x2) 2.50 (x1) 0.50 0.09 26
...
252.27 0.74 PE L1153 MATMUL psS<-wu,xT 128*128 128x128 f32 x2
...
257.75 0.44 PE L1153 MATMUL psS<-wu,xT 128*128 128x128 f32 x2
```

**Twenty dispatches ahead.** Forecast 0 (bounds -1 and 2), measured 1.7 us in after (0.5 to 3.8 over the four kernels): the bound held in after, the centre not. So the sum for the profiled span reads 491.2 + 6.4 + 1.8 + 1.7 = 501.1, where the forecast had 8.7 + 2.3 + 0. Too much in the first two terms by 2.3 and 0.5, and too little in the third by 1.7, cancel to 1.1 us; that it came so near is luck in these sizes, not in the mechanism. The wait behind dispatch 24 made the kernel slower; how much slower an execution was also hung on the clock in rows 1 to 5, for which the sum had no term.

**Rivals.** (a) and (b) wanted P at 203 or earlier and are out. (c) happened in the profiled execution. Three of the four executions took 509 to 513, (d)'s time or more, and the long profile of after_prelude12 has the stretched rows and the P of 213 or later that (d) named (sorted rows at 109.33, P at 215.51). Of (d)'s two reasons the filter chain holds, with a clock that falls in it; the dispatches held by products are the small one (1.1 us in after). The change did what it says.

## What to carry to other kernels

A queue that is started earlier can lose all its gain if an instruction of the critical path has been moved further back in it: count from the queue's start to that instruction, and from the path to its inputs, and take the later. Before moving work into a covered stretch, compare the cover (here 3.44 us) with everything else that the same change takes from it. A low clock shows in whichever matmuls run first behind an idle stretch, so look for its price there and not only in the group that showed it before. When a change widens the spread of times, compare one profile of each by stage before trusting a median.

## What the runs showed of the hardware that was not expected

Executions of the same one-core kernel differed by 8 to 11 us with the new front part (norm18: nine at 493.7 to 495.8, four at 503.5 to 505.2; front_only: one at 483.85, five at 492.2 to 494.9), and by 4.4 with the old (before: 25 executions in 490.8 to 495.1). Between profiles of either kind 5.9 us stand in rows 1 to 5, where the granted clock is 0.50 for longer; that it makes the whole distance is not shown, since each kernel has one profile. Filling the idle stretches moved the low clock in filt04_busy and removed it from 52.5 to 115 us in front_busy, whose six executions stay within 4.6 us; which stretch does what stays open. One indirect DMA issued by POOL took 6.35 to 6.37 us beside VectorE's radix pass in five profiles, and at most 2.25 beside the same pass in norm18; the reason is open.
